# Late keys and values of a four-layer Flamingo block: stored narrower, with four buffers, and the fourth layer's maxima 32 units ahead

## The reference

```
for layer in (L0, L1, L2, L3):
    x = x + tanh(g_xattn[layer]) * attention[layer](x, context)
    x = x + tanh(g_ffn[layer]) * ffn[layer](x)
```

## Time and profile before

| what | us |
|---|---|
| median of 3 runs | 881.52 (877.07, 881.52, 884.06) |
| the profiled execution | 890.45, its span 888.7, mean granted TensorE clock 0.927 |
| busy in the span: PE | 758.9 (85%) |
| busy: DVE | 611.2 (69%) |
| busy: ACT | 415.3 (47%) |
| busy: POOL | 332.2 (37%) |

### The profile page before, as it was taken

One profiled execution on the slowest core, in us unless ns is written; L12 is line 12 of the kernel. 1 busy time (PEld: TensorE's weight loads), 2 busy tenths in 40 slices (PEclk: granted clock), 3 DMA queues, 4 the chain that ended last, 5 costly groups with the idle time before them and its releaser, 6 DMA issues.

```text
span 888.7 us, 15989 instructions
## 1 busy us (share of the span) xinstructions
PE 758.9 (85%) x5636; PEld 500.2 (56%) x5636; DVE 611.2 (69%) x1270; ACT 415.3 (47%) x698; POOL 332.2 (37%) x269
## 2 busy tenths in 40 slices
PE   4699999974676678999699999998689999988996
PEld 4577777764444347664355555564336666554664
DVE  4789999994687425655656655557689999815652
ACT  2566666670454242452354454531027777654331
POOL 1765555550533440254087777750140000000111
PEclk9899999987888975999799999999959999999999
DMA  7366766423517533020504222207604565500220
GB/s 196 105 216 230 255 224 204 134 75 103 91 53 222 168 125 89 28 80 26 140 19 120 78 72 72 72 1 100 143 1 123 126 171 135 152 1 24 80 98 22
DMA packets 56610, 97.18 MB, mean 109 GB/s; under 512 B 16970, under 2 KB 41034, under 8 KB 55226
## 3 DMA queue, kind: packets, MB, share of 16 engines
q1 hardware_dynamic: 56546, 96.32, 38.0%
HBM read 64.65 MB, written 31.65 MB: 108 GB/s over the span
## 4 chain that ended last, share of the span: by engine, by line
PE 41%; DVE 32%; DMA 8%; ACT 6%; POOL 5%; issue 4%; SPq 3%; POOLq 0%; DVEq 0%; ACTq 0%
DVE arena L2324 8%; PE ps L1106 8%; DVE arena L1730 7%; PE ps L1096 6%; DMA d_v<-arena 5%; DVE rn L1885 4%; DVE arena L1934 3%; PE ps L1039 3%; PE ps L1274 2%; PE ps L1284 2%; PE ps L1209 2%; DVE arena L1913 2%; PE ps L1198 2%; DVE arena L1893 2%; ACT arena L1535 2%
## 5 line engine op out<-in xcount | busy, mean ns | idle before, releaser
L2324 DVE TENSOR_REDUCE arena<-ps 112x1 f32<-112x500 f32 x192 | 115.5, 669 | 15.1 <-PE ps L1183 14.2
L1730 DVE TENSOR_TENSOR arena<-ps,arena 128x448 f32<-128x448 f32 (+7 forms) x138 | 83.3, 628 | 60.5 <-ACT arena L1558 19.4
L1700 POOL TENSOR_TENSOR arena<-arena 125x448 f32<-125x448 f32 x96 | 109.6, 1142 | 24.1 <-ACT arena L1512 21.1
L1535 ACT ACTIVATE arena<-ps 125x896 f32<-125x896 f32 x96 | 87.0, 917 | 27.0 <-PE ps L1198 26.4
L1106 PE MATMUL ps<-arena 125*128 125x448 f32 (+1 forms) x208 | 97.0, 548 | 1.6 <-ACT arena L1512 1.2
L1592 POOL TENSOR_TENSOR arena<-arena 112x4 f32<-112x4 f32 x9 | 9.3, 1029 | 232.7 <-DVE arena L1754 226.7
L1512 ACT ACTIVATE arena<-arena,kbias 125x448 f32<-125x448 f32 x96 | 63.7, 668 | 65.3 <-DVE arena L1730 46.3
L1730 DVE TENSOR_TENSOR arena<-ps,rn 125x448 f32<-125x448 f32 x96 | 59.3, 618 | 47.7 <-PE ps L1096 43.3
L1096 PE MATMUL ps<-arena 128*125 128x448 f16 (+3 forms) x312 | 77.6, 359 | 3.0 <-DVEq L1741 3.0
L1096 PEld LDWEIGHTS ps<-arena 128*125 128x125 f16 (+1 forms) x312 | 40.8, 135 | 57.2 <-issue 42.3
L794 PE MATMUL ps<-w_k2h,arena 128*125 128x512 f16 x288 | 67.6, 387 | 6.1 <-ACT arena L1344 6.1
(11 more groups left out here) (308 smaller groups left out, 1477.3 us busy)
## 6 DMA issues: line engine op xcount, KB each, us to landing
d_k<-arena SPq DMA_DIRECT2D x24, 375.0 KB
d_v<-arena SPq DMA_DIRECT2D x24, 375.0 KB
arena<-d_k SPq DMA_DIRECT2D x96, 93.8 KB
arena<-d_v SPq DMA_DIRECT2D x8, 1008.0 KB
arena<-in_ctxT SPq DMA_DIRECT2D x8, 750.0 KB, 10.3
d_cln<-arena SPq DMA_DIRECT2D x8, 750.0 KB
d_clnT<-arena SPq DMA_DIRECT2D x8, 750.0 KB
arena<-d_clnT SPq DMA_DIRECT2D x8, 750.0 KB
```

Of the source, the lines that this page charges most:

```text
L1535: act.activation(p3[t % 2].rearrange("p (k h) q -> p k (h q)", k=2), ps[0:KP, 2 * (t % 2):2 * (t % 2) + 2, 0:8 * S], ACT.Exp).then_inc(l3_ ...
L1700: ins = pool.tensor_tensor(psum2[p][0:rows], psum2[p][0:rows], pexp[(t + p) % 2][0:rows], ALU.add)
L1730: return dve.tensor_tensor(out, a, b, op)
L2324: dve.tensor_reduce(mx3[bn % 2][:, u % 2, u % 8 // 2, u // 8:u // 8 + 1], ps[0:TT, max_bank_of(bn, u), 0:500], AX.X, ALU.max).then_inc(l3_ ...
```

## The change

Five edits belong together.

1. **Late keys and values.** `d_k3` holds two rows per key dimension (rounded key, remainder) in place of three (the rounded key twice), and `d_v3` holds the values without gaps. POOL's second copy and ACT's second values copy go. When L3 reads the keys back (`load_keys3`), 16 DMAs per batch in place of 12 put the rounded key twice into the tile; a new `spread_values3` on POOL copies the values into the tile with gaps, once per batch.
2. **Buffers.** Four sets of tiles in place of three; L3's key tile has three buffers in place of two.
3. **L1's context rows** come turned from the host (`c56T`), so the four transposes L861 and ACT's copy go. L1's weights are loaded in the context pass. The stores of units 8 and 9 stand behind the `d_att` store and reload. Unit 15 moves from the middle of L0's feed-forward to behind it.
4. **L3.** Batch 0's masked queries are made by DVE straight from PSUM, the copy of all queries is ACT's. Maxima run 32 units ahead in place of 28, `sim3(b+1, 0)` is issued in the last step of batch b, the turning of the maxima stands two steps earlier, both shift-row copies are ACT's.
5. **The last expert** of L1 and of L3 is added by DVE (`weigh_last`) in place of POOL.

The diff, cut to its core:

```diff
-                sel[src, 0, g, 32 * hh + 8 + 3 * d] = 1.0
-                sel[src, 0, g, 32 * hh + 9 + 3 * d] = 1.0
-                sel[src, 1, g, 32 * hh + 10 + 3 * d] = 1.0
+                sel[src, 0, g, 32 * hh + 8 + 2 * d] = 1.0
+                sel[src, 0, g, 32 * hh + 9 + 2 * d] = 1.0
+                sel[src, 1, g, 32 * hh + 24 + d] = 1.0
+SETS = 4
+MAX_AHEAD = 32
-        d_k3 = nc.dram_tensor("d_k3", (B, 4, 4, 24, C), F16).ap()
-        d_v3 = nc.dram_tensor("d_v3", (B, KP, KT * 192), F32).ap()
+        d_k3 = nc.dram_tensor("d_k3", (B, 4, 4, 16, C), F16).ap()
+        d_v3 = nc.dram_tensor("d_v3", (B, KP, KT * D), F32).ap()
...
             def store_later(u):
-                (b, third), h = UNITS[u], u % 3
+                (b, third), h = UNITS[u], u % SETS
                 sp.wait_ge(l_lo, u + 1)
-                sp.wait_ge(l_dup, u + 1)
...
-            store_later(8)
             sp.wait_ge(l0_att, 1)
...
-            store_later(9)
             sp.wait_ge(l0_st, 16)
...
-            for u in range(10, 13):
+            for u in range(8, 13):
                 store_later(u)
...
+            for b in range(B - 2):
+                if b + 3 < B:
+                    sp.wait_ge(l3_s0, KT * b + 4)
+                    sp.wait_ge(l3_s, KT * b + 4)
+                    load_keys3(b + 3, b % 3, 0)
+                sp.wait_ge(l3_v, b + 1)
+                load_values3(b + 2, b % 2)
...
-            pe.wait_ge(l1_ld, L1_LOADS * 16)
-            for t in range(NT):
-                last = pe.transpose(ps[0:D, 0, TT * t:TT * t + TT], c56[:, t, :], ident[0:TT, 0:TT])
...
-            later(16, 17, 18)
+            later(15, 16, 17, 18)
...
+                    elif b + 1 < B:
+                        sim3(b + 1, 0)
+                    for n in range(2):
+                        ahead = 2 * (KT * b + t) + MAX_AHEAD + n
+                        if ahead < 24 * B:
+                            max_sim(ahead // 24, ahead % 24)
+                    if t == KT - 3 and b + 1 < B:
+                        turn_maxima(b + 1)
...
-                if u >= 3:
-                    act.wait_ge(st_l[h], 32 * (u // 3))
-                if u:
-                    act.wait_ge(l_lo, u if u < B else u - 1)
+                if u >= SETS:
+                    act.wait_ge(st_l[h], 32 * (u // SETS))
+                if u >= 2:
+                    act.wait_ge(l_lo, u - 1)
...
-                pool.tensor_copy(k3[:, 2, :], k3[:, 0, :]).then_inc(l_dup, 1)
...
+            def spread_values3(b):
+                p = b % 2
+                pool.wait_ge(l3_ldv[p], 32 * (b // 2 + 1))
+                if b > 1:
+                    pool.wait_ge(l3_pv, KT * (b - 1) + 2)
+                ch.step(pool.tensor_copy(v3s[p][:, :, 0:D].rearrange("p j (g c) -> p j g c", c=32)[:, :, :, 0:24],
+                                         v3c[p][:, :, 0:96].rearrange("p j (g c) -> p j g c", c=24)))
+                ch.link(pool.tensor_copy(v3s[p][:, :, D:].rearrange("p j (g c) -> p j g c", c=16)[:, :, :, 0:HD16],
+                                         v3c[p][:, :, 96:D].rearrange("p j (g c) -> p j g c", c=HD16)))
+                pool.nop().then_inc(l3_v, 1)
...
+            def weigh_last(k, e, weight, first):
+                dve.wait_ge(ex_acc, first + e + 2)
+                residual(k, y2)
+                weigh(e, 1, weight, first)
+                dve.wait_ge(ex_w, first + e + 3)
+                residual(k, big[:, :, D:2 * D])
```

More of the change, by code:

```diff
@@ L112 @@
 N_LOADS = 12
-L1_LOADS = 5
+L1_LOADS = 4
+SETS = 4
 SQ = 6
@@ L1374, in context @@
                     deviation(b + 1)
-                if first:
-                    act.wait_ge(v3_ones, 6)
                 at = a_uses(b)
@@ L1406, in _ @@
                 act.wait_ge(wsum_in, 1)
+            later(8)
             act.wait_ge(l1_kv, 1)
-            act.copy(c56T, ps[0:D, 0, 0:N]).then_inc(l1_ak, 1)
-            later(8)
-            act.wait_ge(l1_kv, 2)
             act.activation(k1T, ps[0:D, 1, 0:N], ACT.Identity, bias=w_col1[:, 1:2]).then_inc(l1_ak, 1)
@@ L1678, in _ @@
             ch.link(pool.memset(y2, 0.0))
-            with pool.Fori(0, E1 // 2) as i:
-                for p in range(2):
-                    e = 2 * i + p
-                    pool.wait_ge(ex_acc, e + 2)
-                    add_expert(e, p)
+            for e in range(E1 - 1):
+                pool.wait_ge(ex_acc, e + 2)
+                add_expert(e, e % 2)
             rsqrt()
```

256 lines of the change are left out of this document (122 added, 134 removed).

## The result

The changed kernel took 858.91 us (median of 4 runs, 855.38 to 860.95) beside 882.79 us for the kernel before on the same chip: a ratio of 0.9695, 95% interval 0.9648 to 0.9743. Timed again later it took 857.72 (855.93 to 864.45) beside 888.28: 0.9668, 0.9629 to 0.9708. So it is faster by 3.0 to 3.3%, 24 to 31 us. The forecast was 838.6, 42.9 us less. Its direction was right; 858.91 lies 0.9 above the upper end of 858, the ratio on the median of 881.52 (854.6) inside.

The account below looks back on a forecast made before the run. No one engine was taken to bound the whole; waits for loads, the d_att trip and stores stood out. Terms summed to 42.9 us: 890.45 to 847.5 profiled, 838.6 as a median, range 827 to 858.

Parts of the forecast that it names:

- Weights and rows: Ahead of L0's weighing: PE's 9.38 us wait and four transposes (1.01) go; 9.4 us saved, bounds 7.8 and 10.4.
- The d_att trip: L0's attention result to DRAM and back, 16.33 us: stores of units 8 and 9 no longer in it, 4.5 us saved.
- the cap of 6.1: At the d_att trip: DVE, busy until 237.93, then waits 6.1 us, so no more than that can be won.
- Later units: Units 16 to 23 around L1's scores, no longer held by stores: 5.5 us saved before z's turning, 11.7 behind it.
- The clock from 331.4 to 354: End of L1's attention, at granted clock 0.50: some of it may get 1.0; 2 us saved, bounds −3 to 8.
- The rival by which the clock stays up: Clock stays up in 331.4 to 354: 6 us more gained, 832.6 us; chance 0.10.
- The head of L3: Before L3's first maximum: DVE makes batch 0's mask from PSUM, replacing its copy and POOL's mask; 2.9 us saved (2.4 to 3.1).
- L3's batches: L3's attention: DVE's shift-row copy (0.60) and wait (0.64) go, 0.8 us per batch, seven times; 5.6 saved, bounds 0 and 8.7.
- L3's batches give nothing: Rival: the banks of the maxima and PE's 14.95 us set L3's batch pace; 5.6 lost, 844 us; chance 0.13.
- The experts' end: L3's last expert: POOL's last addition (1.26 us) goes, 1.3 us saved; L1's last expert 0.
- From the profile to the median: Whole kernel: profiled 890.45 us stood 8.9 above the 881.52 median; differences taken over unchanged, giving 838.6.
- The slower side: Rival: POOL's spreading of values gates each L3 batch; 883 us at 22 us each, 897 at 24; chance 0.05, slower or same.

Follow-up runs that it names:

- the four kernels: Changed kernel with later shift-row copies, 851.05 us; with value-tile clearings apart, 855.98; with both, 848.18; with both and extra PE multiplications in L3's first maxima, 858.13.
- the later copies: Changed kernel with ACT's two shift-row copies behind step 10 of a batch in place of step 9: 851.05 us, ratio 0.9597.
- the clearing apart: Changed kernel with POOL's clearing of the two spread-value tiles split, one behind each inverse square root after L2's attention: 855.98 us, ratio 0.9615.
- the weights behind the pass: Changed kernel with L1's weights and host-turned context rows loaded behind the context pass, PE waiting ahead of the weighing: 865.60 us, ratio 0.9755.
- the two experiments on it: Changed kernel with L1's weights and turned rows behind the pass, 865.60 us; with all of part three but unit 15 undone, 868.37 us.
- The second profile: The kernel before, unedited, profiled again: 886.07 us, on a chip where its median was 887.2.

## Why the prediction was right in its direction and too large

**Weights and rows, forecast 9.4, got 6.4: too large by 3.** PE's wait went, and the weighing came 8.4 earlier (218.06 to 209.69). DVE lost two waits by it, 7.8 for the weighing and 2.0 for L0's attention behind unit 8 on PE. Three things took 3.6 of this back: the pass ended 0.65 later; PE's products ahead of the weighing took 3.42 in place of 2.05, their clock at 0.50 from 206.95 on where it had been 1.00; and L1843 took 2.84 in place of 1.28. The step that failed is "the weighing that DVE waited for stands right behind the transposes": what stands on DVE around the weighing, and not behind PE's wait, was not added up. The clock's part is a matter of the execution: in the four kernels with the later copies, the clearing apart or both, which are the same up to here, the products took about 2.05, and from the pass's last sums to the first division it was 12.15 us, against 13.52 here and 20.55 before, so 8.4 were won. L1843 lies beside POOL's clearing L1636 (213.63 to 214.68), as L1801 does beside its clearing; with the weights behind the pass the clearing lay beside the next operation, L1847, which then took 2.70 in place of 0.96, while L1843 kept its 1.28. The cause of PE's wait was also more than the order of the loads, as the two experiments on it show. (The 9.4 was called the middle of 7.8 and 10.4, which is 9.1.)

**The d_att trip, forecast 4.5, got 6.2.** The trip went from 16.33 to 10.17. That this is the cap of 6.1 is chance: DVE's other work also ended earlier, so its wait only fell from 6.11 to 1.10, and the cap did not bind. I held the neighbouring stores for the cause and priced them at 5.1; they are, but through unit 8's lateness. With the inputs changed, the stores small but left around the trip, it took 11.02, so the stores' place adds little; the stores moved with the inputs left as before was not run.

**Later units, forecast 5.5 + 11.7, got 6.1 + 12.8.** The step held, each within 1.1 us, and unit 23 was taken 31.4 us earlier (329.75 to 298.32; about 31 announced). L1's scores stood 3.8 to 5.0 us apart, not at the 2.4 named as a sign. Of the two helps it is the smaller stores: three sets lose nothing, 750 KB in four transfers lose 10. That sets and bytes act together, as I argued, was not needed. Whether the bytes or the number of transfers count is not separated. The Trainium skill, "DMA: Bandwidth & Descriptors", section "Why a DMA increments its semaphore by 16 and not by 1", was cited for the values' store on 5 engines; no trace here shows how many engines a store runs on, and the share of 0.48 does not tell it either. What the traces show is when a store lets ACT go on: 13 to 16 us after its issue for units 17 to 23 before, 5.2 and 8.3 with three sets and smaller stores.

**The clock from 331.4 to 354, forecast 2, got 1.7.** The size is right because the clock fell only 2.5 us into the stretch; the first group of weighted values ran ahead of the fall. The rival by which the clock stays up fell twice: in the change itself (0.55) and with PE given more to do (0.61, and slower). Its premise, that the fall came behind waits, does not hold after the change, where PE was busy for 0.88 of the stretch ahead of it. The Trainium skill, "TensorE: Matmul & The Clock Gate", Part 1, has activity release the lower level. The trace agrees in part: the level rose at 326.4, 1.4 us into the 128x512 products L728, but the stretch ahead of it, with PE busy for 18.72 of 23.03 us, did not raise it, and in both places where extra matmuls were put in they cost more than they gave back.

**The head of L3, forecast 2.9, got 3.3 and lost 2.1 ahead of it.** The new clearings on POOL were costed at nothing and not even named. POOL was idle there, but a DVE operation stood still through them. That is a step that failed too, a term put at nothing.

**L3's batches, forecast −5.6, got +1.9: the largest miss, 7.5 us.** Two steps failed. The first is "the copy and the wait go from DVE", so 0.8 per batch. They did go. But I counted the second copy on ACT by its 0.52 and the hold on a bank, and not by what stands behind it in ACT's order: the wait for the turned maxima, 1.29, and the copies, with the exponentials of the next step behind them. One step later on ACT the same edit gives 14.86 a batch, 0.9 less than the shorter batches before, and the whole attention is 5.0 us shorter than before, near the 5.6. The second is that the four more maxima ahead of the first scores were put at nothing: they are the +1.9. My rival "L3's batches give nothing" had the right outcome with the wrong cause (banks and PE's 14.95). Of the 2.1 that the windows ahead of the last one won in all, the last one took 1.8 back (19.78 in place of 17.97), with PE's stop of 2.3 us and a clock of 0.83. "It lies under the batches" was said of the loads of keys and values; the loads of the experts' weights behind them come about 16 us earlier against the end of the attention (51.4 us ahead of it in place of 35.7), and whether they make the stop is open.

**The experts' end, forecast 1.3, got 0.7**, by the end of the span against L3's end, other small things included.

**From the profile to the median, forecast "unchanged", which was wrong by 2 to 9 us.** The profiled execution was 8.9 above the median, and I carried the difference over whole. The second profile shows that executions of the kernel before differ by 6 us in just the wait that the change takes away. So a typical execution had less to win there than the one I read: 24 to 31 us by the medians against 32.8 by the profiles.

**The slower side.** Spreading the values takes 1.15 + 0.51 = 1.66 us on POOL per batch, where I bounded it by 6.8, and POOL then waits 14.2 us for PE; it never decides.

## What to carry to other kernels

When an operation moves to another engine, price it by what it waits for and by what stands behind it in that engine's order, not by its own duration: two copies of 0.5 us cost 1 us of every batch and, moved by one step, nothing. Work that is moved ahead to be out of the way later also has to be paid once, at the start: four maxima more cost 1.9 us. Where a stall is set by how transfers fall together, a single profile is one draw of it; before carrying a gain over to the median, see whether the profile's excess lies in the very wait that the change removes. And a short idle moment that recurs may cost twice, in the wait and in the clock that falls behind it; the traces show the two together in four kernels, and in five others the wait alone.

## What the runs showed of the hardware

- A tensor-scalar operation of DVE (0.17 us by itself) lasted 2.23 through a POOL clearing of 125x2304, while a reduce beside the first clearing kept its 0.69. With the large clearing ended at its start it took 0.31. Three of 128x512 took 2.84 in place of 1.28 beside a POOL clearing of 128x1152.
- With two row-wise loads (rows of 512 bytes) and a unit's store ahead of them, PE waited 6.01 us for the last load behind them; with one transfer of 128 rows and the store behind, 1.52.
- The same L3 batch, with the same instructions and waits, ran at a granted clock of 1.00 (15.82 us) in five profiles and of 0.90 (17.1 to 17.3) in most batches of four others, all from one chip.
- Extra matmuls where the clock is at its lower level did not raise it enough to pay: 0.55 to 0.61 for 4.8 us lost, and 0.67 to 0.55 for 10.
- PE stopped for 2.0 to 4.3 us with nothing to wait for in all twelve profiles of kernels with the change, while four loads of the experts' weights were in flight; in the two of the kernel before 1.6 and none. What it waited for is not shown.
